# Cross-attention of a decoder layer: each score chunk made in two halves, with a piece's transposes and weighting between them

## What is computed

```
qh = split_heads(x @ Wq);  kh = split_heads(context @ Wk);  vh = split_heads(context @ Wv)
sim = einsum('hid,hjd->hij', qh, kh) * SCALE
mean = mean(sim, axis=-1);  sim = (sim - mean) * 1.5 + mean
attn = softmax(sim, axis=-1)
out = einsum('hij,hjd->hid', attn, vh)   # heads joined again
return einsum('bni,iq->bnq', out, Wout) + bout
```

## Time and profile before

| | us |
|---|---|
| median of 3 runs | 2608.7 |
| the runs | 2606.54 to 2611.08 |
| span of the profiled execution | 2603.9 |
| TensorE busy | 2543.7 |
| weight loads busy | 2283.5 |
| VectorE busy | 1914.2 |
| ScalarE busy | 1606.5 |
| GpSimd busy | 158.2 |

### The profile page before, as it was taken

The page is one execution under the profiler, slowest core; times in us unless marked ns, Lnnn a source line. Parts: engine busy times, 40 slices in busy tenths (PEclk is TensorE's granted clock), DMA queues, the critical chain, the costliest instruction groups (busy, mean ns, idle before and its releaser), DMA issues. The chain is left out here.

```text
span 2603.9 us, 47026 instructions
## 1 busy us (share of the span) xinstructions
PE 2543.7 (98%) x17647; PEld 2283.5 (88%) x17647; DVE 1914.2 (74%) x3606; ACT 1606.5 (62%) x3049; POOL 158.2 (6%) x208
## 2 busy tenths in 40 slices
PE   8999989999999999999999999999999999999998
PEld 6899868998899889988999899988998899889987
DVE  5888767776777677767777777767776777677787
ACT  6899646555666555565566466656665566556566
POOL 1344220000000000000000000000000000000003
PEclk9999999999999999999999999999999999999999
DMA  8765350001100120011000300020001200110001
GB/s 246 211 162 147 101 221 25 17 17 65 66 17 25 57 74 17 16 66 65 25 16 15 116 17 16 17 108 31 17 17 57 74 17 16 65 68 17 28 1 33
DMA packets 60638, 155.47 MB, mean 60 GB/s; under 512 B 8849, under 2 KB 22353, under 8 KB 60465
## 3 DMA queue, kind: packets, MB, share of 16 engines
q1 hardware_dynamic: 56464, 140.15, 16.7%
q0 software_dynamic: 3248, 12.72, 1.6%
q10 hardware_dynamic: 752, 0.26, 0.0%
HBM read 125.70 MB, written 27.39 MB: 59 GB/s over the span
## 5 line engine op out<-in xcount | busy, mean ns | idle before, releaser
L1731 ACT CAST pt_hi<-xt_ps 128x512 fp32r<-128x512 f32 x1024 | 592.4, 585 | 568.9 <-PE xt_ps L1698 553.0
L1810 DVE TENSOR_TENSOR pt_lo<-xt_ps,pt_hi 128x512 fp32r<-128x512 f32 x1024 | 704.4, 688 | 255.4 <-ACT pt_hi L1731 252.1
L1799 DVE TENSOR_SCALAR_CACHE_REDUCE xprobs<-xs_ps 128x1024 f32<-128x1024 f32 x512 | 626.6, 1224 | 176.1 <-PE xs_ps L1638 171.4
L1709 PE MATMUL xo_ps<-pt_hi,v_hi 128*128 128x256 f32 x2048 | 647.3, 316 | 2.4 <-DVE pt_lo L1810 2.3
L1737 ACT ACTIVATE xprobs<-xprobs,xneg_max 128x1024 f32<-128x1024 f32 x512 | 591.4, 1155 | 27.2 <-DVE xneg_max L1805 27.2
L1698 PE MATMUL xt_ps<-ident,xprobs 128*128 128x128 f32 x4096 | 603.7, 272 | 0.0
L1709 PE MATMUL xo_ps<-pt_hi,v_lo 128*128 128x256 f32 x2048 | 571.3, 279 | 0.0
L1709 PE MATMUL xo_ps<-pt_lo,v_hi 128*128 128x256 f32 x2048 | 570.0, 278 | 0.0
L1698 PEld LDWEIGHTS xt_ps<-ident,xprobs 128*128 128x128 f32 x4096 | 484.1, 140 | 61.9 <-issue 6.7
L1709 PEld LDWEIGHTS xo_ps<-pt_hi,v_hi 128*128 128x128 f32 x2048 | 386.3, 189 | 5.7 <-DVE pt_lo L1810 2.6
L1709 PEld LDWEIGHTS xo_ps<-pt_lo,v_hi 128*128 128x128 f32 x2048 | 388.3, 190 | 2.0
(11 more groups left out here) (251 smaller groups left out, 2736.3 us busy)
## 6 DMA issues: line engine op xcount, KB each, us to landing
v_split<-ctx_split SPq DMA_DIRECT2D x68, 768.0 KB, 5.8
xq<-x_split SPq DMA_DIRECT2D x64, 512.0 KB, 3.2
q_st<-rel_split SPq DMA_DIRECT2D x32, 256.0 KB, 3.8
q_st<-q_split SPq DMA_DIRECT2D x32, 192.0 KB, 4.6
k_st<-k_split SPq DMA_DIRECT2D x32, 192.0 KB, 4.7
ctx_split<-ctx_out POOLq DMA_DIRECT2D x8, 768.0 KB, 4.1
q_split<-attn_late SPq DMA_DIRECT2D x8, 512.0 KB, 4.0
k_split<-attn_late SPq DMA_DIRECT2D x8, 512.0 KB, 5.5
```

The lines of the kernel that those rows point to most:

```text
L1709: last = pe.matmul(o_ps[:, 0:GQ], v[:, vs], pt[:, c % 3, GQ * j:GQ * (j + 1)], start=c == 0 and j == 0 and m == 0, stop=c == PIECES - 1 an ...
L1731: act.copy(pt_hi[:, c % 3, :], t_ps[:, c % 3, :]).then_inc(t_rounded, 1)
L1799: dve.tensor_scalar(probs[:, par if kind == "A" else 1 - par, t, CHUNK * i:CHUNK * (i + 1)], s_ps[:, buf, :], LOGIT, None, ALU.mult, ALU.m ...
L1810: dve.tensor_tensor(pt_lo[:, c % 3, :], t_ps[:, c % 3, :], pt_hi[:, c % 3, :].bitcast(F32), ALU.subtract).then_inc(t_ready, 1)
```

## The change

TensorE makes a chunk's three passes for one bank, then later the three passes for the other bank. A new item ("half",) stands one piece ahead of the chunk's own item; TensorE does the first bank there, and the second where the chunk's item stands. VectorE and ScalarE have nothing at a half; they meet the chunk at its own item. `scores_at` places a half and its chunk on neighbouring pieces. So the chunks move: A(0,3) from piece 0 to halves at 0 and 1, A(1,0) from 2 to 2 and 3, A(1,1) from 4 to 4 and 5, A(1,2) from 6 to 6 and 7, A(1,3) from 8 to 8 and 9, A+(0,0) from 12 to 11 and 12, A+(0,1) from 14 to 13 and 14, A+(0,2) from 15 to 15 and 16 (between W 14 and W 15), and in step 8 the four chunks from 6, 8, 10, 12 to 5 and 6, 7 and 8, 9 and 10, 11 and 12. The number of matmuls and weight loads is the same; the wait for the buffer stands at the first half. A common step on TensorE becomes T 0, half, T 1, half, T 2, W 0, half, T 3, W 1, half and so on; at piece 7 the second half is followed by Q+, and piece 10 has out and no half. The chunks of the head's first step stay whole.

```diff
-    return items + [("W", PIECES - 2), ("W", PIECES - 1)]
+    return items + [("W", PIECES - 2)] + extra.get(PIECES, []) + [("W", PIECES - 1)]
...
-SCORES = {0: [("A", 0, 3)], 1: [("M", 0), ("I",)], 2: [("A", 1, 0)], 4: [("A", 1, 1)], 6: [("A", 1, 2)],
-          8: [("A", 1, 3)], 9: [("M", 1)]}
+def scores_at(first, *which):
+    return merged(*({first + 2 * n: [("half",)], first + 2 * n + 1: [item]} for n, item in enumerate(which)))
+
+
+SCORES = merged(scores_at(0, ("A", 0, 3), ("A", 1, 0), ("A", 1, 1), ("A", 1, 2), ("A", 1, 3)),
+                {1: [("M", 0), ("I",)], 9: [("M", 1)]})
 EXPS = merged(exponents(0, 3), exponents(1, 10))
-AHEAD = {7: [("Q+",)], 12: [("A+", 0, 0)], 14: [("A+", 0, 1)], 15: [("A+", 0, 2)]}
+AHEAD = merged({7: [("Q+",)]}, scores_at(11, ("A+", 0, 0), ("A+", 0, 1), ("A+", 0, 2)))
...
-STEP_8 = with_pieces({0: [("K+", 2)], 1: [("I",)], 2: [("K+", 3)], 4: [("out",)], 6: [("A", 0, 0)],
-                      8: [("A", 0, 1)], 10: [("A", 0, 2)], 12: [("A", 0, 3)], 13: [("V+", 4)], 15: [("V+", 5)]}, [("O",)])
+STEP_8 = with_pieces(merged({0: [("K+", 2)], 1: [("I",)], 2: [("K+", 3)], 4: [("out",)], 13: [("V+", 4)], 15: [("V+", 5)]},
+                            scores_at(5, ("A", 0, 0), ("A", 0, 1), ("A", 0, 2), ("A", 0, 3))), [("O",)])
...
-            def scores(t, i, par, buf):
+            def scores(t, i, par, buf, b):
+                k0 = CHUNK * i + BLK * b
                 for m, (q, k) in enumerate(((q_hi, k_hi), (q_hi, k_lo), (q_lo, k_hi))):
-                    for b in range(2):
-                        k0 = CHUNK * i + BLK * b
-                        last = pe.matmul(s_ps[:, buf, BLK * b:BLK * (b + 1)], q[:, par, P * t:P * (t + 1)], k[:, k0:k0 + BLK],
-                                         start=m == 0, stop=m == 2)
+                    last = pe.matmul(s_ps[:, buf, BLK * b:BLK * (b + 1)], q[:, par, P * t:P * (t + 1)], k[:, k0:k0 + BLK],
+                                     start=m == 0, stop=m == 2)
                 return last
...
+            def score_chunk(item, s, par, chunk, n, buf, halves):
+                ahead = item[0] == "A+"
+                if halves == (0,):
+                    pe.wait_ge(freed, chunk + (n - 1))
+                if item[1:] == (0, 0) and 0 in halves:
+                    pe.wait_ge(q_ready, s + (2 if ahead else 1))
+                for b in halves:
+                    last = scores(item[1], item[2], 1 - par if ahead else par, buf, b)
+                return last
...
+                    if kind == "half":
+
+                        chunk_item = next(later for later in items[at:] if later[0] in IS_CHUNK)
+                        score_chunk(chunk_item, s, par, chunk, n, (chunk_par + n) % 2, (0,))
+                        halved = True
+                    elif kind in IS_CHUNK:
+                        buf = (chunk_par + n) % 2
+                        if not halved and (items is not BEFORE or n >= 2):
                             pe.wait_ge(freed, chunk + (n - 1))
...
+                        if kind in ("A", "A+"):
+                            last = score_chunk(item, s, par, chunk, n, buf, (1,) if halved else (0, 1))
+                            halved = False
```

More of the change, by code:

```diff
@@ L1653, in project_out @@
                 return last
+            def score_chunk(item, s, par, chunk, n, buf, halves):
[7 more added lines that the diff above has]
+                return last
             def run(items, h, g, s, par, chunk, chunk_par):
                 n = 0
-                for item in items:
+                halved = False
+                for at, item in enumerate(items):
                     kind = item[0]
-                    if kind in IS_CHUNK:
-                        if items is not BEFORE or n >= 2:
-                            pe.wait_ge(freed, chunk + (n - 1))
[L1662 to L1670, removed]
+                    if kind == "half":
[5 more added lines that the diff above has]
+                        if not halved and (items is not BEFORE or n >= 2):
+                            pe.wait_ge(freed, chunk + (n - 1))
+                        if kind in ("A", "A+"):
+                            last = score_chunk(item, s, par, chunk, n, buf, (1,) if halved else (0, 1))
+                            halved = False
                         elif kind == "Q+":
```

## The result

| | before | after |
|---|---|---|
| median of 21 runs, us | 2607.24 | 2610.04 |
| runs, us | 2603.6 to 2611.49 | 2608.39 to 2617.02 |
| span of the profiled execution, us | 2603.9 | 2615.2 |
| TensorE busy in it, us | 2543.7 | 2555.3 |
| mean granted clock in it | 0.999 | 0.995 |

The medians differ by 2.8 us and the means by 3.7; the ratio over all runs is 1.0014, interval 1.0008 to 1.002: slower. That is inside the 0.2% of the sum's case and inside the range of 2597 to 2614, but on the other side of the forecast of -2.6 us, and the interval leaves no change out.

A forecast was written before the change was run, and what follows sets the result against it. TensorE's own matmul time was taken as the bound. Weightings -0.4 and halves' pace -2.7, plus 0.5 for switches and 0 for waits, gave -2.6 us: 2608.7 to 2606.1 us, range 2597 to 2614 for 8 in 10.

The forecast's parts named there:

- the sum's case: Whole kernel: time within 0.2%, 5.2 us, of the kernel before, with -2.6 us as the sum; chance 0.58.
- Bank order: Score chunks: three matmuls in a row into one bank instead of neighbours alternating between two; cost 0.
- One more change from transposes to scores: Each split step on TensorE: one more switch to score matmuls costs about 0.01 us, at most +0.5 us over 56 steps.
- The margin at piece 8: First half of A(1,3), which needs A(1,2) read out by VectorE: 0.28 us left, so no wait, cost 0.
- If a half acts as a chunk does: Weightings on TensorE: short and long alternate, giving 356 short against 339, so -0.4 us.
- the halves' own pace: Score halves on TensorE: some 360 follow a short weighting and gain 0.01 us each, -2.7 us, between 0 and -8.
- The halves spoil it: Weightings on TensorE: every one becomes long, +7.8 + 0.5 us, so 2617; chance 0.08.
- The halves lift the pace: Weightings and halves on TensorE: up to 468 more short weightings, nearly all halves start fast, down to -19 us; chance 0.24.
- A new wait: Piece 8, first half of A(1,3) behind VectorE's read-out of A(1,2): 56 times the overrun, e.g. +9.5 us, 2616; chance 0.08.
- Hidden headroom: Score weight loads on TensorE: their idle time could be spent on neighbouring weightings, up to -125 us; chance 0.02.
- the bounds for that: Weightings on TensorE: all long again gives +7.8 us, all 807 behind a half or output projection short gives -10.8 us.
- The 4.8 us "around the span": Profiled execution before: its span lies 4.8 us below the median of 2608.7, taken as time around the span and left alone.

The follow-up runs named there:

- 3 + 3: The changed kernel itself, each chunk's six score matmuls cut into three and three, against the kernel before: 2610.04 us, ratio 1.0014.
- 2 + 4: The changed kernel with two of a chunk's six score matmuls in the first part and four in the second: 2605.46 us, ratio 0.9994 to the kernel before.
- 1 + 5: The changed kernel with one of a chunk's six score matmuls in the first part and five in the second: 2614.6 us, one run.
- 5 + 1: The changed kernel with five of a chunk's six score matmuls in the first part and one in the second: 2616.83 us, one run.
- quiet ScalarE: Exponentials cut to 64 of 1024 columns, in the changed kernel and the one before: 2598.78 and 2595.43 us, beside 2610.88 before, one run each.

## Why the prediction was wrong

Right, and by which row: TensorE bounds the common steps and waits for nobody in them (the stretch from 1230 that was called the five steps holds most of step 1 too; the five common steps, 1252.65 to 1406.62, show 153.97 of 153.97). Bank order costs nothing (339 short and 30.794 us with it). One more change from transposes to scores costs about 0.01 us (first halves behind transposes 0.784 instead of 0.702, less 76 ns in the transposes). A half takes 0.702 behind a long weighting and 0.689 to 0.693 behind a short one, the 0.01 that was priced. The margin at piece 8 held (the first load there starts 0.31 us behind the end of the read-out in the common steps), and the split that spends it pays.

The step that failed is "If a half acts as a chunk does, short and long alternate, 79% of the times that they can". A half at its new place doesn't. After a long weighting with a half between, 206 of 514 were short, 40%; after one with the output projection between, 15 of 56 (55 of 56 before). Nor does a whole chunk that stands at the second half's place (100 of 252). So the 79% belonged to the order of the kernel before, and not to what a chunk is. "After a short one, long" held, in all 134 places with a half between. So 221 short ones came instead of the 356 worked out. Term by term, from the first to the last transposes:

- The weightings: -0.4 forecast, +1.3 measured. 118 fewer short ones at 0.024 would be +2.8, but long and short have both become 1 to 2 ns shorter, which gives back half of it.
- The scores with their transposes: -2.7 for the halves' own pace and +0.5 forecast, +0.4 measured. 360 halves behind a short weighting were forecast; there were 206. At the measured 0.011 each, less the 88 chunks of before at the same, that is -1.3. Against it, the 538 halves behind a long weighting take 0.702 each where half of a whole chunk took 0.700 (1.401 in all): +0.9. The prediction put that at nothing ("leaves the sum unchanged").
- The Q projection has no term in the sum. It moved from behind a short weighting to behind a half, 684 to 710 ns, 48 times: +1.2.

The output projection gives back 0.2 and the V projections add 0.2. That makes +2.8 instead of -2.6.

The rivals. "The halves spoil it" had the right sign, and a third of its price: 118 of 339 short weightings went, not all. "The halves lift the pace" went the wrong way. "A new wait" didn't come in 3 + 3. "Hidden headroom" didn't show: the weight loads' busy share fell, from 141.44 to 140.19 of 154 us, while the steps grew longer. By the rule of the Trainium skill (Perfetto Trace Analysis, Identifying the Most-Contended Engine) a lower share is more room; the traces don't agree, since the kernel with the lower share has the longer step.

The chances: 0.58 lay on "within 0.2%", where the ratio came out, but the time named was on the wrong side of no change. A share read off six matmuls between two weightings was carried over to three with nothing in the trace that had three; the bounds for that (+7.8 to -10.8) were the honest statement, and the value inside them was a guess with a row behind it. The 4.8 us "around the span" were mis-sized too: the profiled execution after is 2617.02 us with a span of 2615.2, so 1.8 us lie around it, and the other 3.0 were the distance of that execution from the median. It doesn't touch the difference.

What stays open: what in TensorE sets the short or the long state. The runs exclude the bank order, ScalarE's exponentials and VectorE's rests. VectorE's read-outs and the rest of ScalarE's work were not taken away; but the split 2 + 4 has the same lists for both engines as 3 + 3, and another step. The runs show that the cut decides, that the step of one program is the same in every execution that was traced, and that no rule on even or odd counts covers all five cuts. No record shows more than the starts.

## What to carry to other kernels

Where TensorE runs without a gap, a reordering of the same matmuls is worth what their pace is worth, and that has to be measured per order: here the cuts of one chunk lie between -0.07% (2 + 4) and +0.43% (1 + 5) in the step's length; the +0.65% of 5 + 1 has a wait in it. Read such a change from the length of a repeated step, start to start, and not from whole times; two executions differed by 11.3 us, 8.5 of them outside the steps that the change reorders. And when a statistic of the old order ("79% behind a chunk") is the only ground for the new one, list what else sits next to what moves, as the Q projection did here.

## What had not been expected of the hardware

- The pace of TensorE has two levels at full granted clock, 0.112 and 0.118 us per matmul of 256 columns inside a weighting (1334.48 to 1335.04, five of them, against 1337.00 to 1337.59), and which one comes depends on the matmuls ahead, in the common steps the same way in every execution traced of one TensorE list, on two chips. It didn't move when a third of ScalarE's or of VectorE's work was left out.
- The kernels with quiet ScalarE are some 12 to 15 us faster than the kernel before beside them, with the common steps no shorter. Beside the trace of the kernel before, the one with quiet ScalarE is 9.5 us shorter from the first to the last transposes (2142.56 and 2152.08). 8 of these lie between heads: from the first transposes of a head's step 8 to those of the next head's step 1, 57.60 us before and 56.44 with quiet ScalarE, seven times. 1.4 more lie in step 7 of the last head, and the rest of the 12 to 15 is outside the cross-attention's steps and in what differs between executions, with one run each. So the exponentials cost time only in these stretches; the first of them holds the head's unsplit first step, which the change leaves alone. That the cost sits in that step itself was not tried apart.
- The granted clock fell to half outside the cross-attention for a few us at a time, at places that differ between executions (32 to 36 us after: 0.50, where it was 1.00 before; 0.60 at 336 to 340 before). That goes with whole times that differ by more than this change is worth: 7.1 us ahead of the cross-attention between these two traces.
